# Attention in a four-layer graph network: every third batch's last step fetched by SyncE instead of every fourth, and row-end maxima stored by head

## The reference, cut to what matters

```python
def _gat_layer(h, W, al, ar, src, dst, residual):
    feat = (h @ W).reshape(N, H, D)                  # H = 4 heads of 64
    el = jnp.sum(feat * al[None], axis=-1)
    er = jnp.sum(feat * ar[None], axis=-1)
    e = jax.nn.leaky_relu(el[src] + er[dst], NEG_SLOPE)
    m = jax.ops.segment_max(e, dst, num_segments=N)
    ...
    ex = jnp.exp(e - m[dst])
    den = jax.ops.segment_sum(ex, dst, num_segments=N)
    a = ex / jnp.maximum(den[dst], jnp.asarray(1e-09, ex.dtype))
    out = jax.ops.segment_sum(a[:, :, None] * feat[src], dst, num_segments=N)
    ...
```

## Time and profile before

| | |
|---|---|
| median of 3 runs | 6626.07 us (6622.88 to 6629.47) |
| the profiled execution's own time | 6623.83 us |
| its span, first to last instruction | 6622.0 us |
| mean granted TensorE clock | 0.807 of full speed |
| first attention | about 2414 to 3484 us |
| second attention | about 3489 to 4560 us |
| third attention | about 4566 to 5646 us |

### The profile page before, as it was taken

How to read it: one execution, slowest core, us unless ns; L and a number is a source line. 1 busy time by engine, 2 the same in 40 slices (tenths; PEclk the granted TensorE clock), 3 DMA queues, 4 the chain that set the end, 5 groups by cost and what they waited for, 6 DMA issues and landing times. The chain is left out here.

```text
span 6622.0 us, 117574 instructions
## 1 busy us (share of the span) xinstructions
PE 4723.6 (71%) x16858; PEld 2807.9 (42%) x16858; DVE 4472.2 (68%) x11788; ACT 2887.8 (44%) x11591; POOL 4600.5 (69%) x4869
## 2 busy tenths in 40 slices
PE   9977777766777657767775777775677677666666
PEld 4445554543333334444443444443444444333333
DVE  5146566555555578888886888886888888655555
ACT  3310000000000067888875888885788888000000
POOL 0057777767777637777776777777777777677776
PEclk9988888878888877888887888787788877777777
DMA  6444444433333345555544555554555554344443
GB/s 204 160 138 122 123 123 122 122 107 109 109 109 109 106 143 141 142 143 144 141 118 135 142 142 146 142 141 148 139 142 141 142 144 118 102 116 116 117 116 106
DMA packets 446609, 865.78 MB, mean 131 GB/s; under 512 B 121901, under 2 KB 273094, under 8 KB 445866
## 3 DMA queue, kind: packets, MB, share of 16 engines
q0 software_dynamic: 227728, 627.54, 34.6%
q1 hardware_dynamic: 174624, 190.99, 9.1%
q10 hardware_dynamic: 43514, 39.73, 2.0%
HBM read 755.74 MB, written 102.10 MB: 130 GB/s over the span
## 5 line engine op out<-in xcount | busy, mean ns | idle before, releaser
L671 POOL DMA_INDIRECT rows_a<-table,rows_src x2454 | 2350.3, 958 | 882.5 <-issue 530.6
L891 PE MATMUL ps<-rows_a,hot_a 128*128 x4980 | 1858.6, 496 | 776.9 <-DMA rows_a<-table,rows_tile_a 407.6
L2064 ACT ACTIVATE rows_a<-rows_a,ex_a 128x64 f32<-128x64 f32 x9588 | 2321.1, 337 | 0.0
L2141 PE MATMUL ps<-rows_a,hot_a 128*128 128x260 f32 x4908 | 1814.3, 490 | 159.4 <-DVE agg L1973 145.9
L806 DVE TENSOR_TENSOR agg<-agg,ps 128x256 f32 (+1 forms) x2490 | 1045.6, 420 | 1202.4 <-PE ps L891 1130.3
L736 POOL DMA_INDIRECT rows_a<-table,rows_tile_a x1460 | 1383.5, 948 | 445.3 <-issue 257.8
L891 PEld LDWEIGHTS ps<-rows_a,hot_a 128*128 128x128 f32 x4980 | 1026.5, 236 | 1533.2 <-DVE agg L806 866.6
L1973 DVE TENSOR_TENSOR agg<-agg,ps 128x260 f32 x2490 | 1038.4, 417 | 319.0 <-PE ps L2141 130.4
L2141 PEld LDWEIGHTS ps<-rows_a,hot_a 128*128 128x128 f32 x4908 | 973.7, 230 | 449.2 <-issue 342.5
L736 POOL DMA_INDIRECT rows_a<-table,row x759 | 721.0, 950 | 231.6 <-issue 151.4
L2076 PE MATMUL ps<-ident,el_a 128*64 128x128 f32 x156 | 57.1, 366 | 520.1 <-DVE fac_a L1960 507.9
(11 more groups left out here) (355 smaller groups left out, 4165.3 us busy)
## 6 DMA issues: line engine op xcount, KB each, us to landing
rows_a<-table SPq DMA_DIRECT2D x6528, 1.0 KB
dstt_a<-dloc_dram SPq DMA_DIRECT2D x156, 512.0 KB
own_a<-table SPq DMA_DIRECT2D x4608, 1.0 KB
table<-ob SPq DMA_DIRECT2D x48, 1024.0 KB, 4.6
rows_a<-table,rows_src POOLq DMA_INDIRECT x2454
rows_a<-table ACTq DMA_DIRECT2D x2304, 1.0 KB
rows_a<-table,rows_tile_a POOLq DMA_INDIRECT x1460, 3.2
table<-ob_n SPq DMA_DIRECT2D x98, 130.0 KB, 3.0
```

Of the source, the lines that this page charges most:

```text
L671: nc.gpsimd.indirect_dma_start(out=rows[:, n % ring, 0:width], out_offset=None, in_=table, in_offset=bass.IndirectOffsetOnAxis(ap=index[:, ...
L891: nc.tensor.matmul(ps[n % banks][:, 0:width], hot[:, m % nbuf, j, :], mine[n % 4], start=True, stop=True).then_inc(step_done, 1)
L2064: ins = nc.scalar.mul(a, a, ex[:, k % GV, s, h:h + 1])
L2141: nc.tensor.matmul(ps[j % banks][:, 0:W4], hot[:, j, :], step_rows(k, j), start=True, stop=True).then_inc(step_done, 1)
```

## The change

The own step becomes the last step of every third batch: batches 2, 5, ... 47, sixteen an attention instead of twelve. In each batch SP asks for 42, 42 and then 44 rows of it instead of 32, in one load of 32 offsets and a second of 10 or 12. The marks are written once with the four heads side by side, by four strided DMAs in the first stage, and are read with one DMA a batch in place of two. The waits on `flags` count 48 for a batch instead of 64.

```diff
-OWN_BATCH = 4
+OWN_BATCH = 3
...
-    whole_dram = nc.dram_tensor("whole_dram", (2, SP_), FP, kind="Internal").ap()
+    whole_dram = nc.dram_tensor("whole_dram", (SP_ // UG, 2, H, UG), FP, kind="Internal").ap()
...
-                        sp.dma_start(whole_dram.rearrange("(o q) e -> o q e", o=1), wrow[:]).then_inc(whole_out, 16)
+                        for h in range(H):
+                            sp.dma_start(whole_dram[:, :, h, :].unsqueeze(0).rearrange("o k q u -> o q k u"),
+                                         wrow[:].rearrange("o q (k u) -> o q k u", u=UG),
+                                         allow_slow_non_contiguous=True).then_inc(whole_out, 16)
...
-                    for q in range(2):
-                        sp.dma_start(whole[:, v, q, :, 1:UG + 1],
-                                     whole_dram[q:q + 1, k * UG:(k + 1) * UG].unsqueeze(1).to_broadcast([1, H, UG])
-                                     ).then_inc(flags[v], 16)
+                    sp.dma_start(whole[:, v, :, :, 1:UG + 1], whole_dram[k:k + 1]).then_inc(flags[v], 16)
...
                     if k // OWN_BATCH < len(OWN_BATCHES):
-                        own_rows(k // OWN_BATCH, part * (k % OWN_BATCH), part * (k % OWN_BATCH + 1))
+                        own_rows(k // OWN_BATCH, part * (k % OWN_BATCH),
+                                 part * (k % OWN_BATCH + 1) if k % OWN_BATCH + 1 < OWN_BATCH else P)
...
-                    dve.wait_ge(flags[k % GV], k // GV * 64 + 64)
+                    dve.wait_ge(flags[k % GV], (k // GV + 1) * 48)
```

More of the change, by code:

```diff
@@ L371, in _ @@
                 sp.wait_ge(rows_out, 16 * (1 + H))
-                sp.wait_ge(whole_out, 128)
+                sp.wait_ge(whole_out, 16 * (7 + H))
             @block.vector
@@ L552, in _ @@
                 dve.wait_ge(rows_copied, SC)
-                last_of_four = rows_src[:, 0:len(OWN_BATCHES) * OWN_STRIDE].rearrange("p (i e) -> p i e", e=OWN_STRIDE)
-                nc.vector.tensor_scalar(own_src[:], last_of_four[:, :, OWN_STRIDE - 1:].rearrange("p i e -> p (i e)"),
+                last_of_each = rows_src[:, 0:len(OWN_BATCHES) * OWN_STRIDE].rearrange("p (i e) -> p i e", e=OWN_STRIDE)
+                nc.vector.tensor_scalar(own_src[:], last_of_each[:, :, OWN_STRIDE - 1:].rearrange("p i e -> p (i e)"),
                                         4.0 * W4, None, ALU.mult)
@@ L1782, in _ @@
                 k = KG - 1
-                pool.wait_ge(flags[k % GV], k // GV * 64 + 64)
+                pool.wait_ge(flags[k % GV], (k // GV + 1) * 48)
                 pool.wait_ge(er_done, k)
@@ L1892, in within_rows @@
                     v = k % GV
-                    dve.wait_ge(flags[v], k // GV * 64 + 64)
+                    dve.wait_ge(flags[v], (k // GV + 1) * 48)
                     dve.wait_ge(elt_done, k + 1)
```

## The result

The changed kernel takes 7048.23 us (median of 5 runs, 7032.33 to 7057.08) against 6626.07 us before. The ratio is 1.0639, 95% interval [1.0628, 1.0651]: 423 us slower. The forecast of 6750 had the sign and SP as the new bound, but its range of 6695 to 6830 did not hold the time: the cost is 3.4 times what I summed.

The account below looks back on a forecast made before the run. POOL and VectorE together set the pace before; SP, at +4.1 us a batch, becomes the bound. The attentions' 46.6 + 45.0 + 32.0 = 123.6 us on 6623.8 give 6747.4, with 2.2 for the median 6750 us; range 6695 to 6830.

Parts of the forecast that it names:

- SP as the new bound: In the attentions, three batches with stores take SP 63.2 us where VectorE needs 59.7.
- the price of the loads of offsets: On SP, a load of 32 offsets takes 2.20 us; the added second load 1.05, with gaps +1.15 us a batch.
- Rival C: On SP, the second load costs what a full one does, 2.2 us: another 155 us, 6905 us; chance 9%.
- the signs of a wrong size: In SP's profile: the second load or the marks request has another length than taken.
- The layout of SP's times: SP's batches laid out per attention: rows of batch 47 come 46.6, 45.0 and 32.0 us late for VectorE.
- Rows cost 0.33 us each still: On SP, 10.67 more row requests a batch at 0.33 us each: +3.55 us a batch.
- One request of the marks: On SP, one marks request less a batch, 0.58 us and its gap: -0.6 us.
- The writes of the marks at nothing: Four strided writes in the first stage: taken at nothing, bound 0 to 5 us.
- POOL's saving at nothing beside the rest: On POOL, four gathers fewer an attention, 15 us less work, worth that only where POOL sets the pace.
- rival A: SP's requests are hidden and POOL's 15 us of saved gathers count: faster, 6611 us; chance 3%.
- B: SP is slightly slower than the pace but its lead absorbs it: 6613 to 6639 us; chance 3%.
- The rule that I weighed from the Trainium skill: On SP's queue, by this rule the added requests would be nearly free and only POOL's saving would stand.

Follow-up runs that it names:

- cuts44: The changed kernel with its own rows cut 44, 44 and 40 instead of 42, 42 and 44: 6740.53 us, ratio 1.0165.
- old_marks: The kernel before with own rows every third batch, cut 44, 44 and 40, and marks still by two requests: 6821.66 us, ratio 1.0282.
- whole_only: The changed kernel with own rows every fourth batch as before, keeping the marks' new layout and single request: 6633.14 us, ratio 0.9999.
- Rows96: The changed kernel asking for only 96 of each own step's 128 rows, 32 a batch, the other 32 left out: 6626.87 us, ratio 0.9986.
- act_marks: The changed kernel with own rows cut 32, 32, 64 and the requests for dst_t, marks and whole moved from SP to ACT: 6618.97 us, ratio 0.9993.
- cuts_odd: The changed kernel with its own rows cut 41, 45 and 42 instead of 42, 42 and 44: 7338.06 us, ratio 1.1056.

## Why the prediction was wrong, and where it was right

**The step that failed** is the price of the loads of offsets. The first one was carried over at 2.20 us inside the 16.75 us of a batch, and the second was put at 1.05 by the step "No row shows this size. A load of 32 takes 2.20 us ...". I treated a load's time as a function of its size alone. All 144 loads behind the 2.20 began at lane 0, 32, 64 or 96; the new cuts begin at 42 and 74 as well. The rows held no load at such a lane, so neither the 2.20 nor the straight lines applied there. The forecast's 9.75 us for the loads of three batches is 15.6 in the trace. Most of the 5.8 us come from the load that I didn't price anew: the three first loads take 11.0 us where 6.6 was taken, the three second ones 4.6 where 3.15 was. Aligned, the six loads of cuts44 shown above take 9.4 us, and the price that I took for an aligned second load, 1.05, was right: 1.01, 0.79 and 1.20 there (the last is long; its median over 48 own steps is 1.01). Rival C had every second load at 2.2; that is nearly what the one at lane 74 takes (2.32), but the excess of the one at 42, 4.8 us every three batches, was in no rival. Nor was the first load among the signs of a wrong size.

**How the 423 us divide.** 314 us fall with the alignment (cuts44). The other 109 us are what the forecast was about: 124 forecast, 109 (98 to 121 by the interval) measured in cuts44. The layout of SP's times holds for each attention too: the own step of batch 47 was forecast 46.6, 45.0 and 32.0 us late, and in the trace of cuts44 each attention makes it 41.0, 40.2 and 24.3 us later than in the kernel before.

**Right by its own steps.** SP becomes the bound; its waits at `batch(k)` nearly vanish; VectorE waits at the own rows of every third batch; POOL stops at a full ring. Rows cost 0.33 us each still. One request of the marks takes 0.665 us where 0.58 was taken: the two took 1.21 us from first to last, the one takes 0.67. That leaves about 0.5 us saved, not 0.6; old_marks shows it as 0.57. The writes of the marks at nothing: right (whole_only). POOL's saving at nothing beside the rest: right. Rows96 gives what rival A asked for as about 9 us, where A had 15, the end of the interval; that it is less because VectorE sets nearly the same pace fits VectorE's wait for gathered rows there (87.7 us against 92.0), but isn't shown.

**Rivals.** A is refuted as it stood (SP is not hidden), though act_marks shows what it would have needed: 1.65 us a batch off SP's queue. B is refuted by the time, in cuts44 too. SP does have a lead there at the start of the second and third attentions, where VectorE doesn't wait for own rows at three and four of the first five own steps; it is gone after that. The rule that I weighed from the Trainium skill ("DMA: Bandwidth & Descriptors", Issuing engines are not separate DMA queues), that the sequencer's time is "usually small relative to the DMA itself", doesn't carry the conclusion that I drew from it, that added requests are nearly free. In old_marks one request of 0.6 us a batch moves the time by 78 us, because the queue's own sum bounds. That several engines save the sequencer's time agrees with act_marks, where it is worth 88 us.

## What to carry to other kernels

A queue that only issues DMAs is an engine with a budget: write down what one round of it takes, instruction by instruction, register loads included. Compare that with the round of whoever sets the pace before adding to it. A price read from rows holds for the addresses of those rows; when a change moves where a load begins, the old rows don't show its price. Let blocks of offsets that SP loads into registers begin at multiples of four words: here 128 rows over three batches are better cut 44, 44, 40 or 32, 32, 64 than 42, 42, 44.

## What the runs showed of the hardware that was not expected

A load of n words from SBUF into SP's registers has two prices. Where it began at a multiple of four lanes in the unshifted kernels the medians over 48 own steps are 0.79 us for 8 words and 1.01 for 12 (cuts44), and 2.1 to 2.2 for 32: some 0.055 us a word. One or two words past such a lane it took 2.32 us for 10, 2.72 for 12, 2.94 for 13 and 6.7 to 6.9 for 32: 0.2 us a word. An 8-byte shift of the buffer exchanged the two sets, so it is the address that counts.

Aligned counts that are no multiple of four fit in: 9 words take 1.02 us and 10 take 1.22 (medians of cuts_odd and of the changed kernel at lane 32), so 9 cost as much as 12 and 10 cost more. Counted in pieces, a piece being four words while four are left and a single word otherwise, 8, 9, 10, 12 and 32 aligned words are 2, 3, 4, 3 and 8 pieces. Their times are then about 0.35 us and 0.2 to 0.22 for each piece. An unaligned load goes by single words all through: the 32 at lane 42 don't turn fast after the two words to lane 44. That the engine reads so is my reading of these numbers, an estimate and not shown by itself. Loads of a single word elsewhere (L655, 0.27 to 0.84 us on SP) don't follow it closely.

The Trainium skill ("Runtime: NRT & Kernel Launch", Instruction fetch mechanics) gives such loads about 200 ns a register. It says so of loads from HBM; the unaligned loads here, from SBUF, agree with it (0.2 us a word) and the aligned ones take about a quarter of that.
